# Seeding up's PSUM bank with the shared sums in an octonion feed-forward kernel

## The reference

```python
# conditioned channel mixing, then an octonion gated feed-forward, then the residual
y   = einsum('bct,bcd->bdt', x, weights[condition])         # x: (32, 64, 1024)
def oct_ternary_linear(xp, W):                              # W: (8, out/8, in/8)
    scale = mean(|W|)
    Wq = scale * clip(round(W / scale), -1, 1)              # ternary weights
    M  = einsum('jik,jod->koid', S_OCT, Wq)                 # S_OCT: signs of the octonion product
    return einsum('...id,koid->...ko', xp, M)
gate = oct_ternary_linear(y.reshape(B, T, 8, 128), w_gate)  # hidden 2732 = 8 x 341 (and a rest)
up   = oct_ternary_linear(y.reshape(B, T, 8, 128), w_up)
h    = silu(gate) * up
out  = x + oct_ternary_linear(h.reshape(B, T, 8, -1), w_down)
```

## Time and profile before

| | us |
|---|---|
| median of 3 runs | 687.28 (684.57 to 687.62) |
| profiled execution, its time | 687.36 |
| its span, first to last instruction | 685.6 |
| TensorE matmul busy | 651.0 (95%) |
| VectorE busy | 515.2 (75%) |
| ScalarE busy | 332.3 (48%) |
| GpSimd busy | 369.5 (54%) |
| mean granted TensorE clock | 0.985 of full speed |

### The profile page before, as it was taken

The page is one execution under the profiler, slowest core; times in us unless marked ns, Lnnn a source line. Parts: engine busy times, 40 slices in busy tenths (PEclk is TensorE's granted clock), DMA queues, the critical chain, the costliest instruction groups (busy, mean ns, idle before and its releaser), DMA issues. The chain is left out here.

```text
span 685.6 us, 17393 instructions
## 1 busy us (share of the span) xinstructions
PE 651.0 (95%) x7132; PEld 602.7 (88%) x7132; DVE 515.2 (75%) x873; ACT 332.3 (48%) x586; POOL 369.5 (54%) x432
## 2 busy tenths in 40 slices
PE   3589999899999999999999999999999999999987
PEld 3378889798998999899998999999999999988986
DVE  1897866868877697767878687767878687787784
ACT  4755765254444446254553555345453545434530
POOL 1201379348647476367655476375853486465553
PEclk9899999999999999999999999999999999999996
DMA  8200003031001300032000400032000300021001
GB/s 340 66 2 1 1 3 129 1 130 61 1 2 64 128 1 2 2 124 66 2 3 32 157 3 2 2 103 88 1 2 2 123 2 2 2 86 39 2 1 63
DMA packets 10577, 31.52 MB, mean 46 GB/s; under 512 B 3330, under 2 KB 3330, under 8 KB 10370
## 3 DMA queue, kind: packets, MB, share of 16 engines
q1 hardware_dynamic: 9906, 28.81, 12.1%
q10 hardware_dynamic: 592, 1.61, 0.7%
HBM read 22.02 MB, written 8.39 MB: 44 GB/s over the span
## 5 line engine op out<-in xcount | busy, mean ns | idle before, releaser
L1196 PE MATMUL ps<-y_op,gate_table 128*128 128x256 f16 x1408 | 182.1, 275 | 8.3 <-DVE y_op L936 4.2
L1196 PE MATMUL ps<-y_op,up_table 128*128 128x256 f16 x1408 | 179.9, 273 | 0.5 <-ACT up_table L681 0.5
L1196 PEld LDWEIGHTS ps<-y_op,gate_table 128*128 128x128 f16 x1408 | 138.2, 99 | 26.9 <-issue 5.0
L606 POOL TENSOR_TENSOR h_pairs<-h_f 128x256 f32<-128x256 f32 (+2 forms) x128 | 119.6, 963 | 75.5 <-ACT h_f L724 54.6
L1196 PEld LDWEIGHTS ps<-y_op,up_table 128*128 128x128 f16 x1408 | 137.7, 98 | 16.7 <-DVE up_table L852 0.8
L514 POOL TENSOR_TENSOR o_sb<-o_sb,wd_sb 128x256 f32<-128x256 f32 (+1 forms) x150 | 87.4, 617 | 91.4 <-DVE wd_sb L1065 90.2
L606 POOL TENSOR_TENSOR z_f<-h_pairs 128x512 f32<-128x512 f32 (+1 forms) x80 | 102.5, 1302 | 40.5 <-DVE z_op L952 38.6
L1204 PE MATMUL ps<-third_table,y_op 128*128 128x170 f16 x1408 | 108.7, 237 | 0.0
L1204 PEld LDWEIGHTS ps<-third_table,y_op 128*128 128x128 f16 x1408 | 105.1, 97 | 0.3
L1357 PE MATMUL ps<-down_u,z_op 128*128 128x256 f16 (+1 forms) x768 | 93.4, 279 | 2.4 <-DVE z_op L952 2.4
L1357 PE MATMUL ps<-down_c,h_op 128*128 128x128 f16 (+1 forms) x1536 | 93.6, 221 | 0.0
(11 more groups left out here) (95 smaller groups left out, 674.8 us busy)
## 6 DMA issues: line engine op xcount, KB each, us to landing
x_in<-in_x_dram SPq DMA_DIRECT2D x8, 1024.0 KB, 5.2
o_sb<-in_x_dram SPq DMA_DIRECT2D x16, 512.0 KB, 3.5
out_dram<-o_sb SPq DMA_DIRECT2D x15, 512.0 KB, 2.7
h_op<-in_L_ffn_w_gate_dram ACTq DMA_DIRECT2D x3, 512.0 KB, 6.8
h_op<-in_L_ffn_w_up_dram SPq DMA_DIRECT2D x3, 512.0 KB, 7.5
z_op<-in_L_ffn_w_down_dram SPq DMA_DIRECT2D x1, 1536.0 KB, 11.5
out_dram<-o_sb SPq DMA_DIRECT2D x2, 256.0 KB, 2.1
cond_bd<-in_L_cond_weights_dram SPq DMA_DIRECT2D x30, 16.0 KB, 2.9
```

The lines of the kernel that those rows point to most:

```text
L606: return pool.tensor_tensor(dst, a, b, ALU.add if sign > 0 else ALU.subtract)
L1196: mm = pe.matmul(dst, table[m][:, slot, q, :], y_op[:, op, e, :], start=(i == 0 and e == 0), stop=(i == len(terms) - 1 and e == 1))
```

## The change

Up's shared sum (bank_pr's m = 1 part plus or minus q_sb's) no longer goes to p_sb and from there into an add behind up's products. VectorE writes it straight into up's PSUM bank before these products start (seed_up), once for each half of the bank. TensorE's 16 products of up then have no start flag and accumulate onto it. The add into p_sb covers gate alone (256 elements instead of 512), and the add into u_sb is gone. Silu is written to u_sb in SBUF instead of in place, and the product reads up from its bank.

New waits: up's products wait for up_seeded; the seed waits for the bank to be free (the product of two chunks before, or c_added); silu waits for the product before it. In tiles 1 to 7, chunk 0 runs in the order of the other chunks: shared_pair, shared, own. In tile 0, chunk 0 has gate's own, shared_pair, shared, up's own. Two start-up uses of PSUM move to other banks (y's round 3 of tile 0 from bank 2 to 4, a total from 4 to 5), and y_round sets the start flag once per bank.

```diff
@@ bank_y, totals
-            n = [Y_BANK, 0, 1, 2][r] if T == 0 else Y_BANK
+            n = [Y_BANK, 0, 1, 4][r] if T == 0 else Y_BANK
...
-            return ps[:, Y_BANK, TOK:TOK + 1] if m == 2 else ps[:, 3 + m, 0:NQ]
+            return ps[:, Y_BANK, TOK:TOK + 1] if m == 2 else ps[:, 3 + 2 * m, 0:NQ]
@@ ScalarE, chunk
-                    act.activation(bank_r(s, 0), bank_r(s, 0), ACT.Silu, scale=gate_scale(T)).then_inc(silu_ready, 1)
+                    if n > 0:
+                        act.wait_ge(h_ready, n)
+                    if T > 0 and c == 0:
+                        act.wait_ge(z_ready_dve, T)
+                        act.wait_ge(h_turned, 4 * T)
+                    act.activation(u_sb.rearrange("p h t -> p (h t)"), ps[:, 3 * s, :], ACT.Silu, scale=gate_scale(T)).then_inc(silu_ready, 1)
@@ VectorE
+            def seed_up(s, K, sign):
+
+                dst, pr_up, q_up = bank_r(s, 1), bank_pr(s)[:, 1:2], q_sb[:, 1:2]
+                if GAM[K] > 0:
+                    return signed_add(dst, pr_up.broadcast_to([P, 2, TOK]), q_up.broadcast_to([P, 2, TOK]), sign)
+                assert sign < 0
+                signed_add(dst[:, 0], pr_up[:, 0], q_up[:, 0], -1)
+                return signed_add(dst[:, 1], q_up[:, 0], pr_up[:, 0], -1)
@@ VectorE, chunk
+                sign = G2[K // 2] if K % 2 else 1
+                if c > 1:
+                    dve.wait_ge(h_ready, n - 1)
+                elif T > 0:
+
+                    dve.wait_ge(c_added, SUB * (T - 1) + c + 1)
+                else:
+                    dve.wait_ge(y_squared, 4)
+                    dve.wait_ge(y_copied, 4)
+                seed_up(s, K, sign).then_inc(up_seeded, 1)
                 if n > 0:
-                    dve.wait_ge(u_ready, n)
+                    dve.wait_ge(g_ready, n)
                 if T > 0 and c == 0:
+                    dve.wait_ge(u_ready, third(T - 1, NC - 1))
                     dve.wait_ge(z_ready_dve, T)
-                signed_add(p_sb, bank_pr(s), q_sb[:], G2[K // 2] if K % 2 else 1).then_inc(p_ready, 1)
+                signed_add(p_sb[:, 0], bank_pr(s)[:, 0], q_sb[:, 0], sign).then_inc(p_ready, 1)
...
                 dve.wait_ge(up_done, n + 1)
-                if n > 0:
-                    dve.wait_ge(h_ready, n)
-                add_p(u_sb[:], bank_r(s, 1), 1, K).then_inc(u_ready, 1)
...
-                dve.wait_ge(u_ready, n + 1)
-                dve.scalar_tensor_tensor(out=bank_r(s, 0), in0=u_sb[:], scalar=up_scale(T), in1=bank_r(s, 0),
+                dve.scalar_tensor_tensor(out=bank_r(s, 0), in0=bank_r(s, 1), scalar=up_scale(T), in1=u_sb[:],
                                          op0=ALU.mult, op1=ALU.mult).then_inc(h_ready, 1)
@@ TensorE
-            def own(T, c):
+            def own(T, c, m):
...
+                if m:
+
+                    pe.wait_ge(up_seeded, up_chunk(T, c))
+                else:
+                    if T > 0 and c < 2:
+                        pe.wait_ge(c_added, SUB * (T - 1) + c + 1)
...
+                for h in range(2):
+                    mm = group(bank_r(s, m)[:, h], m, [(slots[wr[h, K, p][0]], q, wr[h, K, p][1])
+                                                       for p in range(4)], bool(m))
+                mm.then_inc(up_done if m else gate_done, 1)
 
             def gate_up(T, c):
...
-                if c == 0:
+                if c == 0 and T == 0:
                     pe.wait_ge(y_ready, NY * T + 2)
-                    own(T, c)
+                    own(T, c, 0)
                     pe.wait_ge(y_ready, NY * T + 3)
...
                     shared_pair(T, c)
                     shared(T, c)
+                    own(T, c, 1)
                     return
+                if c == 0:
+                    pe.wait_ge(y_ready, NY * T + 3)
...
-                own(T, c)
+                for m in range(2):
+                    own(T, c, m)
```

More of the change, by code:

```diff
@@ L423, in build @@
         g_ready = sem("g_ready")
+        up_seeded = sem("up_seeded")
         u_ready = sem("u_ready")
@@ L447, in build, with up_chunk, third @@
         NS = 10
+        def up_chunk(T, c):
+            return C3 * T + c + 1
+        def third(T, c):
+            return (NC - C3) * T + c - C3 + 1
         z_dve = h_f[:, NC - 4:NC, 1, :]
@@ L766, in chunk @@
                 if c >= C3:
-                    act.wait_ge(u_ready, n + 1)
+                    act.wait_ge(u_ready, third(T, c))
                     if c > C3 + 1:
@@ L1000, in third_chunk @@
                     h_lo(T, c - 2)
-                dve.wait_ge(u_ready, n + 1)
+                dve.wait_ge(u_ready, third(T, c))
                 dve.wait_ge(silu_ready, n + 1)
@@ L1180, in y_round @@
                         mm = pe.matmul(bank_y(T, r)[:, i, P * s:P * s + P], x_in[:, s, f:f + P], cond_bd[:, s, :],
-                                       start=True, stop=True)
+                                       start=(i == 0 and s == 0), stop=True, skip_group_check=True)
                 mm.then_inc(y_done, 1)
@@ L1191, in row_norms, with group @@
                 mm.then_inc(norm_done, 1)
-            def group(dst, m, terms):
+            def group(dst, m, terms, seeded=False):
                 for i, (slot, q, op) in enumerate(terms):
@@ L1196, in group @@
                         mm = pe.matmul(dst, table[m][:, slot, q, :], y_op[:, op, e, :],
-                                       start=(i == 0 and e == 0), stop=(i == len(terms) - 1 and e == 1))
+                                       start=(i == 0 and e == 0 and not seeded),
+                                       stop=(i == len(terms) - 1 and e == 1), skip_group_check=seeded)
                 return mm
@@ L1283, in shared @@
                 mm.then_inc(pr_done, 1)
[L1285 removed]
+            def own(T, c, m):
                 K, q = CHUNKS[c]
                 n, s = NC * T + c, c % 2
[L1288 to L1303 removed]
+                if m:
+                    pe.wait_ge(up_seeded, up_chunk(T, c))
+                else:
+                    if T > 0 and c < 2:
+                        pe.wait_ge(c_added, SUB * (T - 1) + c + 1)
+                    if n >= 2:
+                        pe.wait_ge(h_lo_ready, n - 1)
+                        pe.wait_ge(h_copied, n - 1)
+                if T == 0 and c % 4 == 0:
+                    pe.wait_ge(slots_built[m], NBUILD * (q + 1))
+                    pe.wait_ge(slots_copied[m], NCOPY * (q + 1))
+                for h in range(2):
+                    mm = group(bank_r(s, m)[:, h], m, [(slots[wr[h, K, p][0]], q, wr[h, K, p][1])
+                                                       for p in range(4)], bool(m))
+                mm.then_inc(up_done if m else gate_done, 1)
             def gate_up(T, c):
```

24 lines of the change are left out of this document (6 added, 18 removed).

## The result

The changed kernel takes 702.38 us (median of 4 runs, 700.42 to 704.1) against 687.26 us for the kernel before, run beside it: a ratio of 1.0228, with a 95% interval of 1.019 to 1.0265. It is slower, by 15.1 us. It is the fastest of the four: its mean granted clock is 0.985, that of the three others 0.980 to 0.981, and their times are 1.8 to 3.7 us longer. No profile shows where these lost the clock.

The account below looks back on a forecast made before the run. The prediction took TensorE, busy 95% of the span, as the bound. To 687.36 us it added 12.6 for seven boundaries, 0.8 for tile 0 and 1.75 for one clock fall: 702.5 us, range 698.5 to 711.

Parts of the forecast that it names:

- What bounds the kernel, and VectorE's saved work: Whole kernel: TensorE, busy 95% of the span, is the bound; 17 us less VectorE time counts for nothing.
- The steady chunk: Tiles 1 to 7, chunks 1 to 7: the seed is ready 0.7 us before up's products need it; cost nothing.
- the remainder of z_lo: Between chunks 5 and 6: z_lo's delay beyond the 0.7 us gained from the earlier h stays inside the cover; nothing.
- The boundary: First chunk of tiles 1 to 7: 40 matmuls can begin only at wd_ready; 1.80 us each, 12.6 us in all.
- the change leaves their work alone: Third window's chunks: unchanged work, so an earlier h would not bring wd_ready early enough; said against the not-slower rival.
- rival 3: Tile ends: earlier h brings wd_ready early enough, from 1.8 us on boundaries cost nothing; 688 us, chance 0.05.
- Tile 0: Tile 0: seeds queue behind table and ternary work, mostly covered by old waits; +0.8 us, bounds 0 and +3.3.
- The clock: Tile boundaries: idle stretches of about 2 us can lower TensorE's clock; one fall counted, at the first boundary, 1.75 us.
- Rival 1: Tile boundaries: the clock falls at three or more; 708 us with four, 713 with all seven; chance 0.20.
- Rival 2: Every chunk: seeds end over 0.7 us later than worked out and stall TensorE; 0.3 us each gives 719 us; chance 0.07.
- Rival 4: Seeded up bank: TensorE overwrites the seed, so the sum is wrong but the time the same; no chance of its own.

Follow-up runs that it names:

- e9_z_later: Changed kernel with VectorE's z_lo behind chunk 5 moved behind gate's add of chunk 6 in tiles 1 to 7; 714.46 us, ratio 1.0426.
- e10_split_tile0_old: Changed kernel with half 1's mix behind the next tile's first seed and no seeds in tile 0 (add in place behind up's products); 687.21 us, ratio 1.0017.

## Why the prediction was right, and where its terms were not

The forecast was 702.5 us with a range of 698.5 to 711; the median is 702.38 us. The direction, the mechanism and the place were right. The closeness of the number is partly luck. The terms found add up to 2 us less than the forecast ones, and some were off in opposite directions; the median lies close because the other three executions, at a lower granted clock, took 1.8 to 3.7 us more than the profiled one. Against the profiled execution, 13.1 us above that of before:

| term | forecast | found |
|---|---|---|
| seven boundaries | 12.6 | 9.7 (1.79 at the first, 1.32 at six) |
| seed of chunk 6 behind z_lo | 0 | 0.8 (6 x 0.14) |
| tile 0, start included | 0.8 | 1.4 |
| clock, first boundary | 1.75 | 2.5 |
| clock, last stretch | 0 | -1.5 |
| sum | 15.1 | 12.9 |

- **What bounds the kernel, and VectorE's saved work.** Right: VectorE lost 14.2 us of busy time (17 forecast), and none of it shortened the time.
- **The steady chunk.** Right for all but one chunk of a tile, and in tile 7 for that one too. No seed shows as a releaser in tiles 1 to 7 with a wait over 0.2 us. The step that failed is the remainder of z_lo, which was said to lie inside the cover. The earlier product moved z_lo onto GpSimd's h_pairs (166.92 to 169.42 us) in tiles 1 to 6, where it takes 1.96 to 1.99 us. In the kernel before it starts at 164.02, when GpSimd's run has ended at 163.71, and takes 1.22. The Trainium skill, "GPSIMD Engine Reference", section "1. Specifications", says that the SBUF interfaces are shared and that VectorE contends there when it has two SBUF inputs. z_lo reads two buffers in SBUF, and the 0.77 us it lost agrees with that.
- **The boundary.** The 8 products ahead, the wait for wd_ready and its releaser were as said, and at the first boundary the size too (1.79 against 1.80). At the other six the term was mis-sized, 1.32 instead of 1.80, since "the change leaves their work alone" was not the whole of it. The earlier h let GpSimd finish sooner, and ScalarE's z_hi and the q_sb copy behind it no longer waited. That is rival 3's mechanism, which gave back 0.47 us and not the 1.8 from which it decides; what stopped it is TensorE's own place in the third window, as the argument against it had said.
- **Tile 0.** The seeds of chunks 1 and 5 waited 2.44 and 3.06 us (forecast some 2.5 and 3), and the wait before 49.93 shrank, clock fall and all. The net term was 1.7 us and not 0.8; its bound was 3.3.
- **The clock.** In the profiled execution a fall came at the first boundary and at no other. It began within the wait (the granted clock is 0.82 from 131 to 132 us and 0.50 from there to 138) and cost 2.5 us, where 1.75 was taken from the shorter low stretch at 49.93. The Trainium skill, "TensorE: Matmul & The Clock Gate", section "Why this matters for your kernels", warns only of idle gaps longer than those at six of the boundaries. In e9_z_later the clock fell behind gaps of 2.08 and 2.36 us, among matmuls of full height, so here the measurement differs from the rule and decides.
- **Rivals.** Rival 1 did not occur in the profiled execution of this kernel but did in e9_z_later, with five falls. Rival 2 is excluded by the 696 ns and the chunks without waits. Rival 3 occurred in a quarter of its size. Rival 4 would have shown no time of its own.

## What to carry to other kernels

Before moving an engine's work ahead of a point, list for each moved instruction which buffer it needs and in which order the other engine frees them: here most of the loss came from the first two instructions of a tile asking for the buffer that is freed last, and one other order of four operations took it back almost whole (1.5 us of wait to 0.2). Work removed from an engine that is not the bound is worth nothing, but it shifts everything behind it, so look where the shifted operations now collide, and keep a wait on a third engine behind, and not ahead of, what the bound needs. Where TensorE idles, a wait that grows from 1.5 to 2.1 us can cost 1.7 us more than its own length, as at five of six boundaries of e9_z_later.

## What was not expected of the hardware

- A gap of the same length is followed by a clock fall in one execution and not in the next: 3.00 us with a fall (133.27 us in the changed kernel) and without one (136.57 us in e9_z_later). Even within one execution, 2.09 us at 217.01 had none and 2.08 us at 379.81 had one, and in e10_split_tile0_old one followed only 1.68 us at 128.85. A fall cost 1.66 us in e9_z_later and 2.5 us at the first boundary of the changed kernel; so kernels that differ by a few microseconds are told apart by their waits and periods rather than by one time.
- A VectorE operation on two SBUF buffers took 1.99 us when its first 0.91 us fell beside a GpSimd operation, and 1.22 us alone; tile 7, with the same order and no GpSimd operation beside it, is the control.
- TensorE accumulates onto values that VectorE wrote into the bank, and neither side shows a price: the 16 seeded matmuls take 1.92 us, the 16 with a start flag 1.91. Matmuls had written both of up's banks, 1 and 4, before the first seed (y's rounds in tile 0, one of which the change moved to bank 4); no run seeds a bank without that.
